# One transfer of 128 partitions in place of two of 48 for each tile's keys and queries, and another order of the passage round the last output product

## Chip, cores and metric

One core of one Trainium2 chip runs the whole program. The metric is device time in microseconds (us) of one execution, and the number that counts is the median of several.

## What is computed

1024 tokens of 512 values pass four layers, each with a residual sum and a layer norm: an attention over the 32 heads of each token by itself, a three-layer dense network, an attention with rotary embedding and a sliding window of 128 tokens, and a mixture of experts (16 experts, the best 2 per token, and a shared expert). The change lies in the third layer and in the step from it to the fourth. Cut to that:

```python
# third layer: 32 heads of 16 values, S = 1024
q, k = rope(heads(x @ Wq.T)), rope(heads(x @ Wk.T))
scores = q @ k.T / 4
scores = where((j <= i) & (j > i - 128), scores, -inf)
x = layernorm(x + (softmax(scores) @ v) @ Wo.T)
# fourth layer begins with
logits = x @ gate_w.T          # 16 experts; top 2 of softmax(logits)
```

## The kernel before

The tokens are 8 tiles (T = 8) of 128. The program is written out by hand: each engine has its own list of instructions, and semaphores tie them. Values kept in fp32 precision are split into a high and a low part (fp32r), and a product is the sum of high x high, high x low and low x high.

**Keys and queries of the third layer.** For a tile t, `rotate` and `rope_sum` (VectorE) apply the rotary embedding to one of the two products, n = 1 the keys and n = 0 the queries. `turn_rotated` (TensorE) transposes the rows, `parts_out_high` (ScalarE) and `parts_low` (VectorE) write the high and the low part. What the score products want is another layout: for each pair `pr` of 16 head pairs, one head's 16 values in three blocks (high, high, low for queries; high, low, high for keys) one below the other, 48 partitions, at partition 0 for one head and at partition 64 for the other (KS = 64). Since partitions change places, this goes through DRAM. `relay_rows` (L856) issues three stores per tile and side on SyncE's queue into `ys`, the DRAM tensor `slots_out` that the fourth layer needs only later; `stack_rows` (L1795) issues two loads per tile and side on GpSimd's queue (L1803), each of 48 partitions with 8 KB in each (384 KB), one for each half. Queries go to `qS` (three buffers, called XR and QS in the profile), keys to `kS` (four buffers, called RP). All of `kS` is set to -1 beforehand (L1792, L1830, L1838), so that the two partitions below the three blocks hold -1.

**Scores.** The main loop (L635 on TensorE) runs i from -1 to 7 with 8 steps s each. In one iteration the stages of several tiles stand side by side: `row_scores(i + 1, s)` (L562, its products are L573) for the row maxima, `key_scores(i, ...)` (L578, products L586) for the exponentials, `weigh` (L601) for softmax x values, `project2` (L515) for the products of tile i + 2, `context_rows` (L546) and `output` for tile i - 1. `row_scores(t, 0)`, the first instruction of an iteration, waits for `stack_in`, that is for the loads of the keys and the queries of tile t. VectorE takes the maxima (`row_maxima`, L1185), splits them, TensorE turns them, and `stack_maxima` (L1810, GpSimd's queue) writes them as two more partitions (48 and 49 of each half) below the queries, so that 50 rows of `qS` and `kS` give score minus maximum. `key_scores(i, 0, 0)` waits for that transfer (`max_in`). ScalarE takes the exponentials, GpSimd cuts the window out of them (`mask`, L1818 and L1821).

On GpSimd, iteration i has in step 4 a mask, then `stack_rows(i + 2, 1)`, in step 5 a mask, then `stack_rows(i + 2, 0)`, in step 6 a mask, then `stack_maxima(i + 1, 0)`, in step 7 a mask.

**From the third layer to the fourth.** After the loop the last tile's context is turned (L546, L553), its output product runs (`output(U, R, 7)`, 12 products of L515), VectorE adds it and takes the statistics (`add_output`), and every tile is normalised (`normalise`, ScalarE) and turned (`turn_x3`, L343) into XT3, split by `high_x3` (ScalarE) and `low_x3` (VectorE). `logits_turned(g)` multiplies the four tiles of group g with the gate (12 products of L332 from RP and XR). Turned tiles go through the ring V, two PSUM banks: a third one waits until VectorE has read the first. The logits decide the slots, and the fourth layer's gathers and weight loads start from those.

The profile calls helpers by their own line: L1451 is every activation, L915 every tensor_tensor, L332 every plain product, L343 a turned row of tiles.

## Time and profile before

| | us |
|---|---|
| median of 3 runs | 733.93 (730.81 to 736.4) |
| the profiled execution | 731.17 |
| its span in the trace | 729.4 |
| mean granted TensorE clock (1 is 2.4 GHz) | 0.918 |
| TensorE busy | 615.2 (84% of the span) |
| VectorE busy | 393.2 (54%) |
| ScalarE busy | 270.8 (37%) |
| GpSimd busy | 239.0 (33%) |

Times in the trace count from the start of the span. The third layer's loop runs from about 230 to 507 us, the step to the fourth layer from there to about 546 us. A row of a timeline gives the start, the duration, the engine, the line, what is written and read, how many instructions are merged, and in brackets how long the engine had been idle before it and what ended that. "<-issue" there means that the profile shows no releaser.

### The profile page before, as it was taken

How to read it: one execution, taken by the hardware profiler on the slowest of the kernel's cores; microseconds unless marked ns; L12 is line 12 of the kernel's file. 1: busy time of each engine (PE TensorE's matmuls, PEld its weight loads, DVE VectorE, ACT ScalarE, POOL GpSimd, SP SyncE). 2: the span in 40 equal slices, each digit the busy share in tenths (PEclk: the TensorE clock that was granted, in tenths of full speed). 3: DMA queues.
4: the chain of work that ended last, by engine and by line, in shares of the span. 5: the costliest groups of instructions: out<-in, count | busy, mean ns of one | idle time of the engine just before them, and what ended most of it. 6: DMA issues, size and time to landing. Idle time of an engine off the chain costs nothing.

```text
span 729.4 us, 13453 instructions
## 1 busy us (share of the span) xinstructions
PE 615.2 (84%) x5108; PEld 485.6 (67%) x5108; DVE 393.2 (54%) x1126; ACT 270.8 (37%) x433; POOL 239.0 (33%) x348
## 2 busy tenths in 40 slices
PE   2998999669889787998979896868789699999985
PEld 2987977557667565666757664645558588888762
DVE  4315445697765775767666684552464133323355
ACT  5155036366563323424243442444530112221313
POOL 6002523543310245535343552462007311111072
PEclk9999999999999886999898997577899899999998
DMA  8921211442057444618171638020007759997455
GB/s 304 392 103 27 54 34 25 104 134 74 0 145 155 106 116 61 155 23 176 35 143 46 131 110 165 2 89 3 0 1 283 279 178 409 415 418 286 185 167 193
DMA packets 49455, 104.37 MB, mean 143 GB/s; under 512 B 12208, under 2 KB 18480, under 8 KB 47856
## 3 DMA queue, kind: packets, MB, share of 16 engines
q1 hardware_dynamic: 30032, 61.68, 24.0%
q0 software_dynamic: 13744, 31.61, 18.9%
q10 hardware_dynamic: 5616, 10.23, 3.9%
q8 instruction: 41, 0.67, 0.4%
q14 instruction: 22, 0.18, 0.1%
HBM read 63.77 MB, written 35.13 MB: 136 GB/s over the span
## 4 chain that ended last, share of the span: by engine, by line
PE 53%; DMA 13%; DVE 10%; ACT 9%; issue 8%; POOL 6%; SPq 1%; POOLq 0%; ACTq 0%; DVEq 0%
PE bank L332 12%; PE bank L515 11%; PE bank L368 9%; DMA slots_out<-FP 5%; ACT FP L1451 4%; DVE FP L915 4%; PE bank L601 3%; PE bank L586 3%; PE bank L573 3%; POOL slots_in L1854 2%; POOL FP L1866 2%; DMA QS<-QS 2%; PE bank L391 2%; PE bank L546 2%; PE bank L379 1%
## 5 line engine op out<-in xcount | busy, mean ns | idle before, releaser
L1451 ACT ACTIVATE FP<-bank 128x512 f32<-128x512 f32 (+1 forms) x244 | 138.7, 611 | 316.3 <-PE bank L586 131.1
L1185 DVE CUSTOM_DVE_ANT_0 kraw<-bank,maskb 128x256 bf16<-128x256 f32 (+1 forms) x256 | 88.5, 401 | 60.1 <-PE bank L573 60.1
L515 PE MATMUL bank<-W,XR 128*128 128x512 f32 x348 | 107.0, 454 | 0.1
L332 PE MATMUL bank<-FP 128*128 128x128 f32 x558 | 89.1, 315 | 1.0 <-ACT FP L1451 1.0
L515 PEld LDWEIGHTS bank<-W,XR 128*128 128x128 f32 x348 | 72.0, 219 | 16.3 <-DVE XR L915 0.3
L368 PE MATMUL bank<-W,XR 128*128 128x512 f32 x288 | 77.6, 419 | 5.2 <-DVE W L915 5.2
L1818 POOL TENSOR_SCALAR_AFFINE_SELECT FP<-FP 128x512 f32<-128x512 f32 x64 | 41.4, 670 | 112.4 <-ACT FP L1451 112.4
L368 PEld LDWEIGHTS bank<-W,XR 128*128 128x128 f32 x288 | 64.2, 271 | 11.8 <-DVE W L915 5.6
L332 PEld LDWEIGHTS bank<-FP 128*128 128x128 f32 x558 | 66.9, 196 | 3.0 <-DVE FP L915 1.6
L915 DVE TENSOR_TENSOR FP<-FP,bank 128x128 f32<-128x128 f32 (+1 forms) x39 | 14.4, 370 | 68.4 <-ACT FP L1451 47.4
L332 PE MATMUL bank<-RP,W 128*128 128x512 f32 x192 | 45.8, 394 | 2.2 <-DVE FP L915 2.2
L1821 POOL TENSOR_SCALAR_AFFINE_SELECT FP<-FP 128x512 f32<-128x512 f32 x56 | 38.0, 705 | 29.3 <-ACT FP L1451 29.1
L1859 POOL DMA_DIRECT2D FP<-slots_in x31 | 16.7, 540 | 86.5 <-PE bank L717 79.9
L1774 POOL DMA_DIRECT2D RPF<-FP x64 | 31.5, 502 | 38.5 <-PE bank L404 27.8
L332 PEld LDWEIGHTS bank<-RP,W 128*128 128x128 f32 x192 | 35.7, 188 | 10.5 <-issue 1.8
L573 PE MATMUL bank<-RP,QS 48*128 48x256 f32 x160 | 23.7, 377 | 22.6 <-issue 11.8
L1386 DVE COPY FP<-bank 128x512 f32<-128x512 f32 x31 | 21.4, 691 | 37.4 <-PE bank L717 37.4
L601 PE MATMUL bank<-FP 128*17 128x128 f32 x960 | 37.9, 308 | 2.0 <-ACT FP L1451 1.8
L915 DVE TENSOR_TENSOR XR<-bank,XR 128x512 fp32r<-128x512 f32 x27 | 21.3, 806 | 31.6 <-ACT XR L1451 31.6
L573 PEld LDWEIGHTS bank<-RP,QS 48*128 48x128 f32 x160 | 14.7, 222 | 34.0 <-issue 24.4
L601 PEld LDWEIGHTS bank<-FP 128*17 128x17 f32 x960 | 26.6, 108 | 13.1 <-issue 6.0
L1854 POOL DMA_INDIRECT slots_in<-X,slots x16 | 16.7, 1045 | 48.1 <-issue 48.1
(168 smaller groups left out, 1019.4 us busy)
## 6 DMA issues: line engine op xcount, KB each, us to landing
FP<-in_experts_dram SPq DMA_DIRECT2D x31, 768.0 KB, 9.6
slots_out<-QS SPq DMA_DIRECT2D x48, 256.0 KB, 2.8
FP<-slots_in POOLq DMA_DIRECT2D x31, 256.0 KB, 6.5
slots_out<-FP ACTq DMA_DIRECT2D x31, 256.0 KB, 8.0
slots_in<-RP SPq DMA_DIRECT2D x7, 1024.0 KB, 13.6
RP<-slots_out POOLq DMA_DIRECT2D x16, 384.0 KB, 6.0
QS<-slots_out POOLq DMA_DIRECT2D x10, 384.0 KB, 8.3
FP<-in_shared_dram SPq DMA_DIRECT2D x4, 768.0 KB, 7.6
```

The lines of the kernel that those rows point to most:

```text
L332: mm = nc.tensor.matmul(bank, lhs, rhs, start=(n == 0), stop=(n == len(terms) - 1))
L368: mm = nc.tensor.matmul(b[:, :], *terms[m], start=(m == 0), stop=(m == 3 * DC - 1))
L515: mm = nc.tensor.matmul(b[:, :], *terms[n], start=(n == 0), stop=(n == len(terms) - 1))
L573: mm = nc.tensor.matmul(both[a][:, m, :], qS[i % 3][half(a, 3 * HD), pr, :], kS[half(a, 3 * HD), slots, pr, :], start=True, stop=True)
L601: mm = nc.tensor.matmul(weighing[32 * q:32 * q + HD + 1, (h // 4 % 4) * P:(h // 4 % 4 + 1) * P], vaug[:, (i - w) % 4, head(h), :], PT[hg % ...
L915: return nc.vector.tensor_tensor(o, a, b, op)
L1185: ins = nc.vector.tensor_tensor_reduce(masked[:, 2 * (f % 2) + m, 0:n], b[:, m, :], maskb[:, m0:m0 + n], 1.0, -BIG, ALU.add, ALU.max, hmax ...
L1451: return nc.scalar.activation(o, i, func, **kw)
L1774: nc.gpsimd.dma_start(vdiag[k % 3][32 * g:32 * g + 32, 272 * g:272 * g + 272].rearrange("p (s d) -> p s d", s=CH), vT[32 * g:32 * g + 32, ...
L1818: ins = nc.gpsimd.affine_select(out=pt, in_=pt, compare_op=ALU.is_ge, fill=0.0, base=0, pattern=[[0, 4], [1, P]], channel_multiplier=-1)
L1821: ins = nc.gpsimd.affine_select(out=pt, in_=pt, compare_op=ALU.is_ge, fill=0.0, base=-1, pattern=[[0, 4], [-1, P]], channel_multiplier=1)
L1854: nc.gpsimd.indirect_dma_start(xs, bass.IndirectOffsetOnAxis(slots[:, k, t:t + 1], 0), X[:, t, :], None).then_inc(scattered, 16)
```

## The change

**One transfer per tile and side.** The relay in DRAM gets a fourth block, so that 32 groups of three partitions become 32 groups of four, and each load is one transfer of all 128 partitions (1 MB in place of twice 384 KB). The fourth block is constant, -1 for keys and 0 for queries: GpSimd sets 32 partitions of two `kS` buffers, and SyncE stores them once into the four places of the relay (`edge_in`). The two partitions of the maxima are now 3 and 7 of each half, a partition of the fourth block each. Both score products now contract over the whole half, 64 rows, in place of 48 and 50. The settings of all of `kS` to -1 go, with two of them inside the loop.

**The passage round the last output product.** The output product of tile 7 stands ahead of all turns of x3 (before: tiles 0 and 1 were turned ahead of it). The turns alternate between ring V and ring Q, four banks in all, six tiles ahead of the first gate product in place of four. ScalarE normalises tiles 0 to 6 in a row. VectorE divides the second half of the last context ahead of the reciprocals for tiles 0 to 6.

```diff
@@ -168,10 +168,9 @@
-        relay_in = [[ys[a:a + 3 * P, :].bitcast(F32R).rearrange("(d m) n -> d (m n)", m=4) for a in (6 * P * n, 6 * P * n + 3 * P)]
-                    for n in range(2)]
-        relay = [[ys[a:a + 3 * P, :].rearrange("(x b m) n -> b x m n", b=3, m=4) for a in (6 * P * n, 6 * P * n + 3 * P)]
-                 for n in range(2)]
+        places = [[slice(4 * P * (2 * n + b), 4 * P * (2 * n + b + 1)) for b in range(2)] for n in range(2)]
+        relay_in = [[ys[rows, :].bitcast(F32R).rearrange("(d m) n -> d (m n)", m=4) for rows in of] for of in places]
+        relay = [[ys[rows, :].rearrange("(x b m) n -> b x m n", b=4, m=4) for rows in of] for of in places]
@@ -212,6 +211,10 @@
         weighing = banks[5]
+
+        def x3_ring(t):
+            return (V, Q)[t % 2]
+
         x_in = [sem(f"x_in{g}") for g in range(2)]
@@ -562,15 +566,15 @@
-                    pe.wait_ge(stack_in[1][i % 2], 32 * (i // 2 + 1))
-                    pe.wait_ge(stack_in[0][i % 2], 32 * (i // 2 + 1))
+                    pe.wait_ge(stack_in[1][i % 2], 16 * (i // 2 + 1))
+                    pe.wait_ge(stack_in[0][i % 2], 16 * (i // 2 + 1))
...
-                        mm = nc.tensor.matmul(both[a][:, m, :], qS[i % 3][half(a, 3 * HD), pr, :], kS[half(a, 3 * HD), slots, pr, :],
+                        mm = nc.tensor.matmul(both[a][:, m, :], qS[i % 3][half(a, KS), pr, :], kS[half(a, KS), slots, pr, :],
@@ -583,8 +587,8 @@
-                        mm = nc.tensor.matmul(both[a][:, m * P:(m + 1) * P], kS[half(a, 3 * HD + 2), (i - w) % 4, pr, :],
-                                              qS[i % 3][half(a, 3 * HD + 2), pr, :], start=True, stop=True)
+                        mm = nc.tensor.matmul(both[a][:, m * P:(m + 1) * P], kS[half(a, KS), (i - w) % 4, pr, :],
+                                              qS[i % 3][half(a, KS), pr, :], start=True, stop=True)
@@ -681,16 +685,16 @@
                     pe.wait_ge(x_ready, 2 * T + t + 1)
-                    transpose_row(("x3", t), X[:, t, :])
+                    transpose_row(("x3", t), X[:, t, :], x3_ring(t))
...
             turn_context(V, U, T - 1)
-            turn_x3(0, 1)
             output(U, R, T - 1)
-            turn_x3(2, 3)
+            turn_x3(*range(T - 2))
             def logits_turned(g):
-                V.drained(pe, ("x3", g * G + G - 1))
+                for t in (g * G + G - 2, g * G + G - 1):
+                    x3_ring(t).drained(pe, ("x3", t))
                 x3 = [[XT3[g][:, a, c, :] for c in range(DC)] for a in range(2)]
@@ -699,7 +703,7 @@
             logits_turned(0)
-            turn_x3(*range(G, T))
+            turn_x3(T - 2, T - 1)
             logits_turned(1)
@@ -857,7 +861,7 @@
                 if t >= 2:
-                    sp.wait_ge(stack_in[n][t % 2], 32 * (t // 2))
+                    sp.wait_ge(stack_in[n][t % 2], 16 * (t // 2))
                 for blk, l in ((0, 0), (1 + n, 0), (2 - n, 1)):
@@ -865,12 +869,17 @@
+            for n in range(2):
+                sp.wait_ge(edge_ready, n + 1)
+                for b in range(2):
+                    sp.dma_start(relay[1 - n][b][3].rearrange("x m n -> x (m n)"),
+                                 kS[0:P // 4, n].rearrange("p a k -> p (a k)").bitcast(F32)).then_inc(edge_in, 16)
             for t in range(T):
...
                     A.filled(sp, ("hidden", 1, 1, DC - 1))
-                    sp.wait_ge(stack_in[0][1], 32)
+                    sp.wait_ge(stack_in[0][1], 16)
                     load_raw(3, ao)
@@ -1286,13 +1295,13 @@
             context_divided(V, T - 1, 0)
+            context_divided(V, T - 1, 1)
             rates(slice(0, T - 1), 5)
-            context_divided(V, T - 1, 1)
             low_dense(("co", T - 1), ca[1], ca[0])
...
                 for t in tiles:
-                    low_xt(("x3", t), [XT3[t // G][:, a, :, t % G * P:(t % G + 1) * P] for a in range(2)])
+                    low_xt(("x3", t), [XT3[t // G][:, a, :, t % G * P:(t % G + 1) * P] for a in range(2)], x3_ring(t))
@@ -1304,12 +1313,12 @@
-            low_x3(0, 1)
             add_output(R, T - 1)
-            low_x3(2, 3)
+            low_x3(0)
             rates(slice(T - 1, T), 6)
+            low_x3(*range(1, T - 2))
             logits_out(0)
-            low_x3(*range(G, T))
+            low_x3(T - 2, T - 1)
             shared_low(2)
@@ -1670,21 +1679,20 @@
             def high_x3(t):
-                high_xt(("x3", t), XT3[t // G][:, 0, :, t % G * P:(t % G + 1) * P])
+                high_xt(("x3", t), XT3[t // G][:, 0, :, t % G * P:(t % G + 1) * P], x3_ring(t))
...
             normalise(0)
-            for t in range(1, G + 1):
+            for t in range(1, T - 1):
                 normalise(t)
-                high_x3(t - 1)
-            for t in range(G + 1, T - 1):
-                normalise(t)
+            high_x3(0)
+            high_x3(1)
             roots(slice(T - 1, T), 6)
...
             normalise(T - 1)
-            for t in range(G, T):
+            for t in range(2, T):
                 high_x3(t)
@@ -1789,25 +1797,22 @@
             for n in range(2):
-                nc.gpsimd.memset(kS[:, n].bitcast(F32), -1.0).then_inc(minus_ready, 1)
+                nc.gpsimd.memset(kS[0:P // 4, n].bitcast(F32), (-1.0, 0.0)[n]).then_inc(edge_ready, 1)
             def stack_rows(t, n):
...
                     Q.filled(p, ("keyscores", t - 3, 7, 1 if t >= 4 else 0))
-                if n == 1:
-                    p.wait_ge(minus_ready, min(t, 3) + 1)
-                rows = relay_in[n][t % 2]
-                for a in range(2):
-                    dst = (qS[t % 3], kS[:, t % 4])[n][KS * a:KS * a + 3 * HD]
-                    nc.gpsimd.dma_start(dst.rearrange("d a q -> d (a q)"), rows[3 * HD * a:3 * HD * a + 3 * HD]).then_inc(stack_in[n][t % 2], 16)
+                if t == 0:
+                    p.wait_ge(edge_in, 64)
+                dst = (qS[t % 3], kS[:, t % 4])[n]
+                nc.gpsimd.dma_start(dst.rearrange("d a q -> d (a q)"), relay_in[n][t % 2]).then_inc(stack_in[n][t % 2], 16)
...
                 for a in range(2):
-                    place = KS * a + 3 * HD
-                    nc.gpsimd.dma_start(qS[t % 3][place:place + 2, 8 * f:8 * f + 8, :],
+                    nc.gpsimd.dma_start(qS[t % 3][KS * a + 3:KS * a + 8:4, 8 * f:8 * f + 8, :],
                                         mxT[HD * a:HD * a + HD, f, :]).then_inc(max_in[f], 16)
@@ -1827,15 +1832,12 @@
             A.filled(p, ("ffn", T - 1))
-            nc.gpsimd.memset(kS[:, 2].bitcast(F32), -1.0).then_inc(minus_ready, 1)
             for i in range(-1, T):
...
                         nc.gpsimd.tensor_tensor(W[:, 7, :], raw_c[3], W[:, 6, :].bitcast(F32), ALU.subtract).then_inc(wo_split, 1)
-                    if (i, step) == (0, 3):
-                        nc.gpsimd.memset(kS[:, 3].bitcast(F32), -1.0).then_inc(minus_ready, 1)
                     if i >= 0 and (step % 2 == 0 or i >= 1):
```

Cut out are the ring arguments of `transpose_row`, `low_xt` and `high_xt` (the ring was always V) and the new semaphores.

GpSimd's list in one iteration (here i = 1, for tile 3; RP is `kS`, XR here `qS`), before:

```order
L1818 AFFINE_SELECT FP<-FP 128x512 x2
L1803 DMA RP<-slots_out 48x2048 x2
L1821 AFFINE_SELECT FP<-FP 128x512 x2
L1803 DMA XR<-slots_out 48x2048 x2
L1818 AFFINE_SELECT FP<-FP 128x512 x2
L1810 DMA QS<-QS 2x8x128 x2
L1821 AFFINE_SELECT FP<-FP 128x512 x2
```

and now:

```order
L1823 AFFINE_SELECT FP<-FP 128x512 x2
L1809 DMA RP<-slots_out 128x2048
L1826 AFFINE_SELECT FP<-FP 128x512 x2
L1809 DMA XR<-slots_out 128x2048
L1823 AFFINE_SELECT FP<-FP 128x512 x2
L1815 DMA QS<-QS 2x8x128 x2
L1826 AFFINE_SELECT FP<-FP 128x512 x2
```

The order is the same; each pair of loads is one load.

TensorE after the loop (from the turn of the last context, L553 before and L557 now, to the second gate product), before:

```order
L553 MATMUL bank<-ident,FP 128x128 x4
L343 MATMUL bank<-ident,X 128x128 x8
L515 MATMUL bank<-W,XR 128x512 x12
L343 MATMUL bank<-ident,X 128x128 x8
L332 MATMUL bank<-RP,XR 16x512 x12
L343 MATMUL bank<-ident,X 128x128 x16
L332 MATMUL bank<-RP,XR 16x512 x12
```

and now:

```order
L557 MATMUL bank<-ident,FP 128x128 x4
L519 MATMUL bank<-W,XR 128x512 x12
L347 MATMUL bank<-ident,X 128x128 x24
L336 MATMUL bank<-RP,XR 16x512 x12
L347 MATMUL bank<-ident,X 128x128 x8
L336 MATMUL bank<-RP,XR 16x512 x12
```

The output product moved ahead of 8 transposes (two tiles), and 8 more moved ahead of the first gate product.

VectorE there, from the first half of the last context to the sum of the output, before:

```order
L1154 RECIPROCAL hsum<-bank 128x16
L915 TENSOR_TENSOR FP<-bank,hsum 128x4x32 x2
L1045 RECIPROCAL rstd<-std 128x7
L1046 SCALAR_TENSOR_TENSOR offset<-mv,rstd 128x7
L1154 RECIPROCAL hsum<-bank 128x16
L915 TENSOR_TENSOR FP<-bank,hsum 128x4x32 x2
L915 TENSOR_TENSOR XR<-bank,XR 128x512
L1299 CAST XR<-FP 128x64
L915 TENSOR_TENSOR XR<-FP,XR 128x64
L1302 MEMSET picked 128x8
L915 TENSOR_TENSOR RP<-bank,RP 128x4x128 x2
L915 TENSOR_TENSOR X<-X,bank 128x512
```

and now:

```order
L1163 RECIPROCAL hsum<-bank 128x16
L924 TENSOR_TENSOR FP<-bank,hsum 128x4x32 x2
L1163 RECIPROCAL hsum<-bank 128x16
L924 TENSOR_TENSOR FP<-bank,hsum 128x4x32 x2
L1054 RECIPROCAL rstd<-std 128x7
L1055 SCALAR_TENSOR_TENSOR offset<-mv,rstd 128x7
L924 TENSOR_TENSOR XR<-bank,XR 128x512
L1308 CAST XR<-FP 128x64
L924 TENSOR_TENSOR XR<-FP,XR 128x64
L1311 MEMSET picked 128x8
L924 TENSOR_TENSOR X<-X,bank 128x512
```

The second division moved ahead of the reciprocals, and the two low parts of x3 moved behind the sum of the output.

## Rows read from the trace of the kernel before

**Rows 1.** Page: the chain of waits by line, share of the span.
```profile
PE bank L332 12%; PE bank L515 11%; PE bank L368 9%; DMA slots_out<-FP 5%; ACT FP L1451 4%; DVE FP L915 4%; PE bank L601 3%; PE bank L586 3%; PE bank L573 3%; POOL slots_in L1854 2%; POOL FP L1866 2%; DMA QS<-QS 2%; PE bank L391 2%; PE bank L546 2%; PE bank L379 1%
```

**Rows 2.** Waits from 184 to 512 us: who waited for whom, us, times, longest.
```profile
PE bank L573 <- issue: 15.1, 5, 6.9
...
PE bank L586 <- DMA QS<-QS: 1.3, 2, 0.7
```

**Rows 3.** Timeline of TensorE where `row_scores(t, 0)` starts, t = 2, 4, 7.
```profile
281.81 0.80 PE L573 MATMUL bank<-RP,QS 48*128 48x256 f32 x4 [2.86 <-DMA QS<-slots_out]
...
347.08 0.56 PE L573 MATMUL bank<-RP,QS 48*128 48x256 f32 x4 [2.52 <-issue]
...
452.93 0.80 PE L573 MATMUL bank<-RP,QS 48*128 48x256 f32 x4 [6.94 <-issue]
```

**Rows 4.** Timeline of GpSimd for tile 4.
```profile
335.27 1.07 POOL L1803 DMA_DIRECT2D RP<-slots_out  x2
...
337.52 1.05 POOL L1803 DMA_DIRECT2D QS<-slots_out  x2
...
341.01 1.18 POOL L1810 DMA_DIRECT2D XR<-QS  x2
```

**Rows 5.** L1803, issue to landing: keys, queries of tile 4; queries of tile 7.
```profile
DMA to landing us min/median/max: 4.8/5.7/6.6
...
DMA to landing us min/median/max: 7.3/8.1/8.9
...
DMA to landing us min/median/max: 10.8/12.9/14.9
```

**Rows 6.** Windows: five engines' busy time, TensorE's clock, mean DMA share, GB/s.
```profile
340.00:341.00 1.00, 1.00 (x13) 0.80 (x11) 0.18 (x2) 1.00 (x3) 1.00 (x2) 1.00 1.03 131
...
344.00:345.00 1.00, 0.55 (x21) 0.27 (x12) 0.96 (x2) 0.38 (x1) 0.00 (x0) 1.00 1.34 180
...
248.00:249.00 1.00, 0.00 (x0) 0.00 (x0) 0.75 (x2) 0.18 (x1) 0.28 (x1) 0.70 1.06 412
...
512.00:519.00 7.00, 6.54 (x23) 5.50 (x24) 2.27 (x7) 3.60 (x6) 0.00 (x0) 0.57 0.00 0
```

**Rows 7.** L1859, four GpSimd loads of 128 partitions issued in a row.
```profile
576.64 2.22 POOL L1859 DMA_DIRECT2D FP<-slots_in  x4 [6.65 <-DMA slots_in<-X,slots]
...
DMA to landing us min/median/max: 3.0/3.5/4.0
```

**Rows 8.** The instructions on RP: min/median/max ns, first and last start.
```profile
L586 PEld LDWEIGHTS bank<-QS,RP x320: 182/188/335, 282.2 to 502.9; 50*128 50x128 f32 x160
...
L332 PEld LDWEIGHTS bank<-RP,W x192: 186/188/192, 534.5 to 703.4; 128*128 128x128 f32 x192
...
L1803 POOL DMA_DIRECT2D RP<-slots_out x16: 512/530/551, 206.9 to 435.7; - x16
...
L1792 POOL MEMSET RP<- x2: 1812/1844/1875, 186.3 to 188.2; 128x2048 f32 x2
```

**Rows 9.** Timelines of TensorE, ScalarE and VectorE after the loop.
```profile
510.42 0.66 PE L553 MATMUL bank<-ident,FP 128*128 128x128 f32 x4 [2.08 <-DVE FP L915]
512.46 1.97 PE L343 MATMUL bank<-ident,X 128*128 128x128 f32 x8 [1.39 <-ACT X L1451]
514.08 4.84 PE L515 MATMUL bank<-W,XR 128*128 128x512 f32 x12
518.76 1.04 PE L343 MATMUL bank<-ident,X 128*128 128x128 f32 x8
530.20 2.94 PE L332 MATMUL bank<-RP,XR 128*16 128x512 f32 x12 [1.48 <-DVE RP L915]
...
511.61 1.51 ACT L1451 ACTIVATE X<-X,offset,rstd 128x512 f32<-128x512 f32 x2
...
509.28 0.20 DVE L1045 RECIPROCAL rstd<-std 128x7 f32<-128x7 f32 x1 [2.49 <-ACT std L1451]
520.51 1.46 DVE L915 TENSOR_TENSOR RP<-bank,RP 128x512 fp32r<-128x512 f32 x2
```

More of the change, by code:

```diff
@@ L930, in _, with low_xt @@
             highs = [0]
-            def low_xt(name, parts):
-                b = V.take(v, name)[:, :].rearrange("p (c n) -> p c n", c=DC)
+            def low_xt(name, parts, ring=V):
+                b = ring.take(v, name)[:, :].rearrange("p (c n) -> p c n", c=DC)
                 hi, lo = parts
```

15 lines of the change are left out of this document (8 added, 7 removed).

## The prediction

> **What bounds the kernel now.** I read the chain of waits by line first. Products on TensorE lead it: L332 12%, L515 11%, L368 9%, L586 and L573 3% each [rows 1]. So TensorE sets the pace, and the question is where it stands idle. The change touches two stretches, and each is read by itself.
>
> The first is the loop. The list of waits for it shows TensorE idle ahead of L573, the row scores, for 15.1 us in 5 waits without a named releaser, and ahead of L586, the key scores, for 1.3 us behind the transfers of the maxima [rows 2]. A sixth wait of L573, 2.86 us, ends with the landing of the queries [rows 3]. The timeline shows where the six stand: at the first product of an iteration, `row_scores(t, 0)`, for t = 2 to 7; three of them are 2.86, 2.52 and 6.94 us [rows 3]. That product waits for the loads of keys and queries of tile t. For t = 4 these loads can be followed. GpSimd issues them at 335.27 (keys, 2) and 337.52 (queries, 2) [rows 4]; the second of the last pair starts half way, at 338.05, and lands 8.9 us later [rows 5], so at 346.9. TensorE starts again at 347.08 [rows 3]. "Issue" in that row is the loads.
>
> I call the issue of the keys T0. TensorE was ready at 347.08 - 2.52 = 344.56, T0 + 9.3; the queries land at T0 + 11.7.
>
> The second stretch is the passage after the loop. TensorE waits 2.08 us for VectorE ahead of the turn of the last context and 1.39 us for ScalarE ahead of the turns of x3; only then does the output product run, in 4.84 us at a mean granted clock of 0.57 [rows 6, 9]. The second gate product starts at 530.20 [rows 9], and everything after it hangs on it, since the logits decide the slots.
>
> **The loads.** The four landings for tile 4 are 335.27 + 4.8 = 340.1, 335.81 + 6.6 = 342.4, 337.52 + 7.3 = 344.8 and 338.05 + 8.9 = 346.9 [rows 4, 5]. They are 2.3 us apart on average: one transfer of 393 KB after the other, at 173 GB/s, and 4.8 - 2.3 = 2.5 us lie ahead of the data of the first. All that time the DMA engines are busy (share 1.03 and more) and move only 131 to 180 GB/s [rows 6]. A load of 128 partitions that runs alone, the output weights on SyncE's queue, moves 412 GB/s at the same share [rows 6]. On GpSimd's own queue four loads of 262 KB and 128 partitions are issued within 2.22 us; the first lands after 3.0 us, the last, issued at about 578.3, after 4.0 us [rows 7], so 786 KB follow between 579.6 and 582.3, 291 GB/s.
>
> One new load has 1049 KB. At 412 GB/s its data take 2.5 us, at 291 GB/s 3.6 us, at 173 GB/s 6.1 us. I take 3.0 us, between the first two, as both are for all 128 partitions. The queries then land at T0 + 2.5 + 3.0 + 3.0 = T0 + 8.5 (T0 + 7.5 to T0 + 9.7), ahead of T0 + 9.3. A single issue also puts the queries' issue at T0 + 1.8 and the maxima's at T0 + 4.7 in place of T0 + 5.7 [rows 4].
>
> The Trainium skill, SBUF — State Buffer, section "Door 1: The DMA port swizzle", says that partitions 0 to 63 reach only half of the 16 ports, that two transfers to the two halves don't add up, and gives 196 GB/s for 64 and 328 GB/s for 128 partitions at 1 MiB. The 173 GB/s above agree with the first; by the second a load would take 3.2 us, the queries would land at T0 + 8.9, and the sum below would stay within half a us.
>
> The maxima follow the queries on the same queue and gate the key scores that start some 0.4 us after `row_scores(t, 0)`; behind the queries they land by T0 + 9.5 to T0 + 11, where TensorE asks for them at T0 + 9.7. I leave 0.3 us of stall per tile. Tiles 2 to 6: the waits are 2.9 + 15.1 - 6.9 + 1.3 = 12.4 us [rows 2, 3], less 5 x 0.3 = 1.5 left over, gain 10.9 us.
>
> Tile 7 is apart: its queries take up to 14.9 us to land [rows 5], because SyncE loads the shared expert's weights at the same time. From about 437.8 us the engines must then move 2.1 MB of keys and queries and 1.8 MB of weights, tables and gate. At 350 to 412 GB/s that is 9.5 to 11 us, to 447.3 to 448.8; TensorE asks at 452.93 - 6.94 = 445.99. Some 1.7 us of the 6.94 stay, gain 5.2 us (3 to 6.9).
>
> Where a stall goes, the next wait shows. During tile 4's stall VectorE works on: 0.96 us of the first microsecond [rows 6]. The first row maxima of an iteration will start about 0.4 us after the scores, and the two banks of V pass that on. Over six iterations I give back 2.0 us (0 to 5).
>
> **What else the first part does, at nothing.** GpSimd sets the constants from 186.3 on, 1.8 us each, and is done at some 190; then SyncE stores them (four stores of 256 KB), by an estimate until 195. The first stack load, which now waits for them (`edge_in`), is issued only at 206.9 [rows 8], behind the first relay, so over ten us cover them. If that cover were gone, one wide load's time, 5.5 us, would bound their cost. The two settings in the loop go, 1.8 us each on GpSimd, off the path. The stores of the relay keep their number and size; their rows lie 32 KB apart instead of 24 KB, which nothing here prices, and tile 4's were landed before its loads were issued; I count it as 0 (0 to 2). The products contract over 64 rows in place of 48 and 50. No row shows 64. A weight load takes 188 ns with 50 rows and 188 ns with 128 [rows 8], so I take 0; if time went with rows, a quarter on top of the 3% and 3% of L573 and L586 [rows 1] would be 11 us.
>
> **The passage.** Step by step with the durations of rows 9. VectorE no longer waits for ScalarE's table and roots ahead of the second division: it starts it when the context is turned, at 508.4, and ends at 509.1 in place of 510.4. The turn of the context ends at 509.8, ScalarE's high part at 510.5, VectorE's low part at 511.2. The output product starts at 511.25. At the low level of the clock it takes 4.5 us, to 515.75, against 518.9 now: 3.2 us early. Then two x3 tiles in 1.04 us, ScalarE 0.6 each, VectorE behind `add_output`, its statistics and the last rates. VectorE has the longest list: sum and statistics 1.6 us to 517.4, low part of tile 0 to 518.1, rates to 518.5, low parts of tiles 1, 2 and 3. ScalarE normalises tile 7 until 519.2 and only then takes tile 2, so tile 2's low part ends at 520.5 and tile 3's at 521.2. First gate product 521.25 to 524.2, tiles 6 and 7 through TensorE, ScalarE and VectorE (0.5 + 0.6 + 0.7 and 0.7 more), second gate product from 526.8 in place of 530.2. Gain 3.4 us. The seven normalisations in a row (some 0.7 us each) [rows 9] end at 515.4, before the first turned tile is wanted by ScalarE. If TensorE, idle for less, keeps the full clock, the output product takes 2.8 us as the gate product's 12 do [rows 9], and the gain is 5.1. If VectorE's list is longer than I have it, 2. What follows (slots, scatter, gathers, experts) starts from there and moves with it.
>
> **Sum.** -10.9 - 5.2 + 2.0 - 3.4 = -17.5 us. The profiled execution took 731.17 us, so it would take 713.7. The median of the runs is 2.8 us above the profiled one, so the forecast is 716 us. The forecast's own range: gains of 10 to 24 us, 709 to 724.
>
> **Rivals.**
> A. *Time goes with bytes.* The new loads carry 33% more. If the 173 GB/s are the way from this DRAM relay or of this queue, and not of the narrow shape, a load takes 6.1 us, the queries land at T0 + 14.7 in place of T0 + 11.7, each of tiles 2 to 6 waits 3 us longer and tile 7 some 4: +19 - 3.4, so 750 us. It decides from 5.3 us per load on. For it: no row shows a load of 128 partitions from the relay with 8 KB rows. Against it: the engines are busy at half the rate of other loads, on the same queue too [rows 6, 7]. The Trainium skill, DMA: Bandwidth & Descriptors, section "Anatomy of one DMA", has a fit of 2.0 us plus bytes over 436 GB/s whatever the shape: 0.9 us for a narrow load and 2.4 for a wide one, so a pair would lose 0.6 us. The 2.3 us between two landings speak against it. Chance 5%.
> B. *The loads get no better.* 1049 KB take as long as two narrow ones, 4.5 us. Only the passage gains: 730 to 731. Chance 7%.
> C. *The stalls go and others come.* Landings are early, but the maxima's transfer, VectorE's list or a cooler clock take half: -8 - 3 = 723 to 727. For it: VectorE is busy in most of the loop, and the maxima's margin is nil. Against it: in the stall both engines run dry. Chance 18%.
> D. The forecast, 70%.
>
> **Chances.** A measurement of this kernel tells about 1% from no change, 726.6 to 741.3. Faster by more: all of D and most of C, 0.86. Within: B, the rest of C and a little of A, 0.09. Slower: A, 0.05. The range that should hold 8 times in 10 takes in D and C: 707 to 727.
>
> **What the changed profile would show.** Loads of 128x2048 with landings of some 5.5 us for the keys, the queries landed some 8.5 us after the keys' issue, 250 GB/s and more in those windows; no wait over 0.5 us ahead of `row_scores(t, 0)` for t = 2 to 6 and one of 1 to 3 us for t = 7; the second gate product some 3.4 us nearer to the last score product. The forecast is wrong if a wide load takes over 5 us of data time, if the idle time reappears ahead of L586 or L1185's bank, or if the products of 64 rows take longer than those of 48.

## The result and the profile after

The changed kernel takes **702.38 us** (median of 4 runs, 696.95 to 709.26) beside 732.37 us of the kernel before on the same chip (4 runs, 730.17 to 736.4): a ratio of **0.956 [0.948, 0.964]**. The ratio leaves out the run of 709.26 us, in which the chip was in its slower state. The forecast was 716 us with a range of 707 to 727. The sign is right, the size is not: the gain is 30 us where 17.5 were forecast, and the time lies below the range.

The profiled execution took 700.95 us, its span is 699.2 us (before 731.17 and 729.4), so the two traces differ by 30.2 us and the medians by 30.0. The page's chain of waits by line, to be held against [rows 1]:

```profile
PE bank L336 17%; PE bank L519 11%; PE bank L372 9%; ACT FP L1460 4%; DVE FP L924 4%; PE bank L605 3%; PE bank L590 3%; PE bank L577 3%; POOL slots_in L1856 2%; PE bank L721 2%; POOL FP L1868 2%; PE bank L395 2%; DVE kraw L1194 2%; PE bank L550 2%; PE bank L383 1%
```

Line numbers have moved: L515 is now L519, the row scores L573 are L577, the key scores L586 are L590, the loads L1803 are L1809. "DMA QS<-QS", the maxima, and "DMA slots_out<-FP" have left the list.

The list of waits from 184 to 512 us, to be held against [rows 2]:

```profile
PE bank L577 <- DVE hmax L1194: 12.6, 14, 2.7
PE bank L577 <- issue: 2.7, 1, 2.7
...
PE bank L590 <- DMA XR<-QS: 1.0, 1, 1.0
```

The lists are cut to the rows of the loads and of the maxima. Five waits of 15.1 us for the loads are one of 2.7. The timeline of TensorE shows where it stands, as [rows 3] did (t = 2, 4, 7):

```profile
280.10 0.80 PE L577 MATMUL bank<-RP,QS 64*128 64x256 f32 x4 [0.75 <-DVE hmax L1194]
...
337.78 0.50 PE L577 MATMUL bank<-RP,QS 64*128 64x256 f32 x4
...
339.02 2.99 PE L519 MATMUL bank<-W,XR 128*128 128x512 f32 x12
...
424.42 0.50 PE L577 MATMUL bank<-RP,QS 64*128 64x256 f32 x4 [2.66 <-issue]
...
425.96 0.66 PE L590 MATMUL bank<-XR,RP 64*128 64x128 f32 x8 [1.05 <-DMA XR<-QS]
```

Tile 4 has no wait at all. Tile 7 still has one, and a second one for its maxima. The timeline of GpSimd for tile 4 and the landings of its keys, its queries and of tile 7's queries answer to [rows 4, 5]:

```profile
328.54 0.59 POOL L1809 DMA_DIRECT2D RP<-slots_out  x1
...
330.66 0.57 POOL L1809 DMA_DIRECT2D QS<-slots_out  x1
...
334.32 1.18 POOL L1815 DMA_DIRECT2D XR<-QS  x2
...
DMA to landing us min/median/max: 5.2/5.2/5.2
...
DMA to landing us min/median/max: 6.9/6.9/6.9
...
DMA to landing us min/median/max: 9.7/9.7/9.7
```

The keys are landed at T0 + 5.2, the queries at 330.66 + 6.9 = 337.6, T0 + 9.0, where they were at T0 + 11.7. The maxima are issued at 334.32, T0 + 5.8, as late as before (T0 + 5.7).

Now the whole loop, for which one list is not enough. The table has T0 of each tile (issue of its keys) and the start of `row_scores(t, 0)`, from the timelines of GpSimd and TensorE. "Load part" is from T0 to the row scores of the same tile, "work part" from the row scores to the next T0.

| t | row scores before | after | load part before | after | work part before | after |
|---|---|---|---|---|---|---|
| 2 | 281.81 | 280.10 | 11.90 | 9.79 | 20.54 | 20.22 |
| 3 | 314.11 | 309.54 | 11.76 | 9.22 | 21.16 | 19.00 |
| 4 | 347.08 | 337.78 | 11.81 | 9.24 | 21.99 | 18.63 |
| 5 | 380.69 | 365.78 | 11.62 | 9.37 | 22.59 | 18.85 |
| 6 | 414.91 | 393.86 | 11.63 | 9.23 | 20.23 | 18.63 |
| 7 | 452.93 | 424.42 | 17.79 | 11.93 | | |

The load parts give 17.7 us, where the forecast counted 16.1 ahead of its give-back. But the work parts, in which nothing waits for a load and for which the forecast had the 1.3 us of the maxima only, give 11.2 more (T0 of t = 2 is 0.4 later: 28.5 in all). Windows of TensorE say what they are. The columns are those of [rows 6]: the window, its length, busy time (and instructions) of TensorE's products, its weight loads, VectorE, ScalarE and GpSimd, then TensorE's granted clock, DMA share and GB/s. Before, the whole stretch from the row scores of tile 2 to those of tile 7, and 4 us behind the stall of t = 4, 5, 6 and 7:

```profile
281.81:452.93 171.12, 146.52 (x1487) 112.36 (x1488) 112.38 (x454) 61.91 (x114) 73.74 (x120) 0.90 0.49 105
...
347.08:351.08 4.00, 4.00 (x20) 3.33 (x21) 2.21 (x11) 1.09 (x2) 1.22 (x2) 0.54 0.00 0
380.69:384.69 4.00, 3.31 (x18) 2.80 (x19) 2.04 (x11) 1.09 (x2) 0.93 (x2) 0.60 0.01 2
414.91:418.91 4.00, 4.00 (x22) 3.39 (x23) 2.21 (x11) 1.08 (x2) 1.22 (x2) 0.59 0.00 0
452.93:456.93 4.00, 4.00 (x29) 3.43 (x29) 2.81 (x14) 1.09 (x2) 1.22 (x2) 0.50 0.00 0
```

And after, the same places:

```profile
280.10:424.42 144.32, 133.24 (x1488) 103.14 (x1488) 113.00 (x456) 61.89 (x114) 70.27 (x111) 0.99 0.42 142
...
337.78:341.78 4.00, 4.00 (x32) 3.32 (x28) 2.89 (x13) 1.69 (x3) 1.22 (x2) 1.00 0.03 6
365.78:369.78 4.00, 4.00 (x27) 3.35 (x28) 2.73 (x13) 1.66 (x3) 1.22 (x2) 1.00 0.01 2
393.86:397.86 4.00, 4.00 (x32) 3.32 (x28) 2.88 (x13) 1.69 (x3) 1.22 (x2) 1.00 0.01 4
424.42:428.42 4.00, 2.95 (x25) 2.27 (x26) 2.40 (x12) 1.08 (x2) 1.03 (x2) 0.81 0.04 10
```

Between the row scores of tile 2 and tile 7 the same products (1487 and 1488 records) keep TensorE busy for 13.3 us less, and it is idle for 11.1 us in place of 24.6, 13.5 less. So half of the 26.8 us is idle time, as expected, and half is the clock: after the waits of 2.3 us and more at t = 4 to 7 TensorE's granted clock was 0.50 to 0.60 in the next 4 us, near the lower level of 1.2 GHz, and where the wait is gone (t = 4 to 6) it is 1.00, that is 2.4 GHz. At t = 4 the order can be seen by the microsecond: the clock is still 1.00 in the last one of the wait (346 to 347), 0.69 in the next, in which TensorE starts again, and 0.50 in those after it, up to 354.

Whole parts of the iteration show where the 13.3 us lie. The work part of tile 4 and the load part of tile 3, before:

```profile
347.08:369.07 21.99, 20.83 (x159) 16.25 (x161) 14.95 (x60) 7.61 (x14) 7.88 (x13) 0.84 0.20 70
...
302.35:314.11 11.76, 10.36 (x143) 7.50 (x141) 7.45 (x32) 4.88 (x9) 6.87 (x13) 0.85 0.99 155
```

and after:

```profile
337.78:356.41 18.63, 17.46 (x165) 13.80 (x161) 15.62 (x62) 8.21 (x15) 7.85 (x13) 1.00 0.21 74
...
300.32:309.54 9.22, 8.80 (x145) 6.62 (x142) 6.58 (x30) 4.27 (x8) 5.91 (x11) 1.00 0.73 242
```

The work parts of tiles 3 to 6, those behind a wait for a load, keep TensorE busy for 80.0 us before and for 70.3 after, 9.7 us less. Their clock was 0.92, 0.84, 0.85 and 0.92 before and is 1.00 in all four after; by these shares the products would have lost 10.2 us, so the clock is enough to explain it. Tile 2's work part gives 0.3 us: it stands at the low level in both kernels (0.50 and 0.57 in its first 4 us). The other 3.1 us are of another kind. In the load parts of tiles 3 and 7 the clock was at 0.50 for some 3 us (from 303 and from 436), behind waits of 0.71 and 0.41 us for VectorE, which stand in nearly every iteration and mostly bring no dip, and with no wait for a load ahead. Such a dip (a short stretch at the low level) in a load part costs 1.6 us and is not bound to the stalls: experiments 3, 4, 5, 6 and 8 have one or two each, the changed kernel's trace has none. So about 10 of the 13.3 us follow the waits for the loads, and 3 may be chance.

The products that stand in the two stretches show the clock as well. The groups of TensorE's products there, before:

```profile
L515 PE MATMUL bank<-W,XR 128*128 128x512 f32 x240 | 73.8, 453 | 0.0
```

after:

```profile
L519 PE MATMUL bank<-W,XR 128*128 128x512 f32 x240 | 64.7, 408 | 0.0
```

240 of the same products keep TensorE busy for 9.1 us less, 453 ns to 408 ns each on average (they overlap).

The passage, to be held against [rows 9]; on TensorE:

```profile
481.82 0.66 PE L557 MATMUL bank<-ident,FP 128*128 128x128 f32 x4 [0.88 <-DVE FP L924]
...
483.96 4.62 PE L519 MATMUL bank<-W,XR 128*128 128x512 f32 x12 [1.48 <-DVE XR L924]
...
494.08 2.93 PE L336 MATMUL bank<-RP,XR 128*16 128x512 f32 x12 [1.59 <-DVE RP L924]
...
499.58 2.94 PE L336 MATMUL bank<-RP,XR 128*16 128x512 f32 x12 [1.69 <-DVE RP L924]
```

The wait ahead of the turn is 1.2 us shorter. From the turn to the second gate product it is 17.76 us where it was 530.20 - 510.42 = 19.78, 2.0 less.

The 30.6 us by which the second gate product is earlier are then: 1.7 at tile 2, 13.5 idle time and 13.3 clock between tiles 2 and 7, 0.1 in iteration 7 (0.7 of busy time, less 0.6 of idle time: 1.2 are saved ahead of the turn, and L590's 1.05 us for the maxima of tile 7, together with longer waits for VectorE, more than take them back), and 2.0 in the passage. 30.2 reach the end.

### The profile page after: what moved, and what is told of

Its sections match the earlier page's. It is cut to its first block, busy times and chain, and to the rows that moved or that the text cites. A ratio compares the mean times of both kernels' runs of the same rounds, so it can differ in the third digit from the quotient of the medians.

```text
span 699.2 us, 13440 instructions
## 1 busy us (share of the span) xinstructions
PE 600.9 (86%) x5108; PEld 475.4 (68%) x5108; DVE 392.0 (56%) x1126; ACT 270.5 (39%) x433; POOL 228.0 (33%) x330
## 4 chain that ended last, share of the span: by engine, by line
PE 60%; DVE 12%; ACT 9%; issue 7%; DMA 6%; POOL 5%; SPq 1%; POOLq 0%; ACTq 0%; DVEq 0%
PE bank L336 17%; PE bank L519 11%; PE bank L372 9%; ACT FP L1460 4%; DVE FP L924 4%; PE bank L605 3%; PE bank L590 3%; PE bank L577 3%; POOL slots_in L1856 2%; PE bank L721 2%; POOL FP L1868 2%; PE bank L395 2%; DVE kraw L1194 2%; PE bank L550 2%; PE bank L383 1%
## 5 line engine op out<-in xcount | busy, mean ns | idle before, releaser
L519 PE MATMUL bank<-W,XR 128*128 128x512 f32 x348 | 99.1, 427 | 1.6 <-DVE XR L924 1.5
L372 PE MATMUL bank<-W,XR 128*128 128x512 f32 x288 | 76.4, 415 | 5.2 <-DVE W L924 5.2
L519 PEld LDWEIGHTS bank<-W,XR 128*128 128x128 f32 x348 | 66.2, 201 | 16.3 <-DVE XR L924 2.0
L372 PEld LDWEIGHTS bank<-W,XR 128*128 128x128 f32 x288 | 63.6, 271 | 11.2 <-DVE W L924 5.6
L605 PE MATMUL bank<-FP 128*17 128x128 f32 x960 | 36.4, 300 | 2.0 <-ACT FP L1460 1.8
L577 PE MATMUL bank<-RP,QS 64*128 64x256 f32 x160 | 22.5, 361 | 12.0 <-DVE hmax L1194 9.1
L721 PEld LDWEIGHTS bank<-ident,FP 128*128 128x128 f32 x124 | 15.8, 145 | 21.3 <-issue 15.7
```

The source lines that it names most:

```text
L372: mm = nc.tensor.matmul(b[:, :], *terms[m], start=(m == 0), stop=(m == 3 * DC - 1))
L519: mm = nc.tensor.matmul(b[:, :], *terms[n], start=(n == 0), stop=(n == len(terms) - 1))
L577: mm = nc.tensor.matmul(both[a][:, m, :], qS[i % 3][half(a, KS), pr, :], kS[half(a, KS), slots, pr, :], start=True, stop=True)
L605: mm = nc.tensor.matmul(weighing[32 * q:32 * q + HD + 1, (h // 4 % 4) * P:(h // 4 % 4 + 1) * P], vaug[:, (i - w) % 4, head(h), :], PT[hg % ...
```

## The experiments

Three questions were open: which part brings how much; whether the clock's part is really a price of the stalls, that a stall has beyond its length; and what made the narrow loads slow (bytes, number of transfers, partitions). The kernels of experiments 1 to 4 ran on one chip, 5 and 6 on a second, 7 and 8 on a third; each is held against runs of the kernel before on its own chip, and ratios are what is compared between them.

### 1. The loads alone

The changed kernel, with the passage as before: one ring, and the order of turns and divisions of the kernel before.

```diff
-                    transpose_row(("x3", t), X[:, t, :], x3_ring(t))
+                    transpose_row(("x3", t), X[:, t, :])
...
-            turn_x3(*range(T - 2))
+            turn_x3(2, 3)
...
-            context_divided(V, T - 1, 1)
...
+            context_divided(V, T - 1, 1)
```

> The changed kernel with the passage after the loop put back as it was before. Theory: the loads took 17.7 us of stalls ahead of row_scores(t, 0) and, because TensorE then kept its full clock after each of those places, another 10.8 us, and the passage only 3.3. So this kernel is some 27 us faster than the one before (about 705), and 3 us slower than the changed one; keys' issue to row_scores(t, 0) stays 9.2 us for t = 3 to 6, and the 12 products behind context_rows take 2.75 us. Rival: the passage brought more than its 3.3 us (its clock, what starts behind it), and the loads only the 16 us that were forecast: then this kernel is at 714 or above.

Measured: 704.99 us (702.41 to 709.45, 4 runs) beside 734.43 of before (19 runs), ratio 0.964 [0.958, 0.970]. From the turn at 482.32 to the second gate product at 501.99 it is 19.67 us, as before. So most of the gain is the loads': 29.4 us, where experiment 4, which has the passage too, gains 32.1.

### 2. The passage alone

The kernel before, with two rings and the new order in the passage (the lines of experiment 1 the other way round).

> The kernel before with only the new passage after the loop; loads as before, two of 48 partitions. Theory: 3.3 us faster than before (some 0.5%), second gate product 3.3 us nearer to the last row_scores(7, 0), everything in the loop as before, with stalls of 2.3 to 2.9 us. Rival: the passage holds part of the unexplained 13 us; then it is 8 us faster or more.

Measured: 730.14 us (723.6 to 737.58, 10 runs) beside 734.43, ratio 0.994 [0.990, 0.999]. That is 4 us, 0.7 to 7.5 by the interval; 3.3 was counted. Its trace has both parts of the passage: 0.88 us of wait ahead of the turn at 517.74 where it was 2.08, and 17.73 us from there to the second gate product (535.47) where it was 19.78. The two changes add up, within what is told apart here: 29.4 + 4.3 = 33.7 beside the 32.1 of both.

### 3. Two transfers of the two halves

The changed kernel, all 64 rows stored and loaded, but in two transfers of 64 partitions each, and so with the bytes of the change and the shape of before (the counts that `stack_in` is waited for double with it).

```diff
-                nc.gpsimd.dma_start(dst.rearrange("d a q -> d (a q)"), relay_in[n][t % 2]).then_inc(stack_in[n][t % 2], 16)
+                for a in range(2):
+                    part = slice(KS * a, KS * a + KS)
+                    nc.gpsimd.dma_start(dst[part].rearrange("d a q -> d (a q)"), relay_in[n][t % 2][part]).then_inc(stack_in[n][t % 2], 16)
```

> The changed kernel, but each load is two transfers of 64 partitions, one for each half (same bytes as the changed kernel, shape as before). Theory (the narrow shape sets the rate): each half moves at some 175 GB/s, 3.0 us apart, the queries land 14.5 us after the keys' issue, stalls ahead of row_scores(t, 0) are 4.5 to 5.5 us for t = 3 to 6, the clock drops behind them, and the kernel is slower than the one before: some 745 to 750 less 3 for the passage. Rival (the number of transfers or some property of the old relay was slow, not the span of partitions): landings stay near 9 us and the time near 702 to 706.

Measured: 734.56 us (730.86 to 740.19, 10 runs), ratio 1.002 [0.998, 1.006]. The whole gain of the loads is gone, and with it what the passage brings. But the expected 742 us and more (745 to 750 less 3) were missed: I had 3.0 us between two landings. The landings of the keys issued at 370.56 and of the queries at 372.81:

```profile
DMA to landing us min/median/max: 5.5/6.5/7.4
...
DMA to landing us min/median/max: 8.0/8.8/9.6
```

The four are at 376.1, 378.5, 380.8 and 382.9 (the second of a pair is issued 0.54 us after the first), 2.3 us apart on average, as in [rows 5] (2.3), with 524 KB in place of 393 KB: about 230 GB/s in place of 173. By the distance of landings a narrow transfer took the same time with 48 partitions and with 64; the first landing is later here in most tiles (5.1 to 5.5 us where it was 4.8 to 5.2 in tiles 2 to 6).

This kernel also shows the clock. (The wait at t = 4 is the shorter one because TensorE comes to it later: its clock had a dip in the load part, as above.) The row scores of t = 4, 5 and 6 on TensorE:

```profile
351.81 0.50 PE L577 MATMUL bank<-RP,QS 64*128 64x256 f32 x4 [1.73 <-issue]
...
383.03 0.51 PE L577 MATMUL bank<-RP,QS 64*128 64x256 f32 x4 [3.19 <-issue]
...
415.99 0.80 PE L577 MATMUL bank<-RP,XR 64*128 64x256 f32 x4 [3.30 <-issue]
```

and 4 us behind each:

```profile
351.81:355.81 4.00, 4.00 (x28) 3.38 (x28) 2.12 (x11) 1.09 (x2) 1.23 (x2) 1.00 0.02 6
...
383.03:387.03 4.00, 4.00 (x23) 3.31 (x24) 2.12 (x11) 1.09 (x2) 1.22 (x2) 0.71 0.00 2
...
415.99:419.99 4.00, 4.00 (x20) 3.58 (x21) 2.21 (x11) 1.08 (x2) 1.22 (x2) 0.50 0.00 0
```

Behind the wait of 1.73 us the clock stays at 1.00 and the work part takes 18.75 us, as in the changed kernel; behind those of 3.19 and 3.30 it is 0.71 and 0.50, and the work part takes 20.38 and 21.53 us. That is the forecast's missing term inside one kernel, with one case of a short wait.

### 4. Two transfers of every other partition

As experiment 3, with the same number of transfers of the same size, but one takes the even partitions and one the odd.

```diff
-                    part = slice(KS * a, KS * a + KS)
+                    part = slice(a, P, 2)
```

> The changed kernel, but each load is two transfers of 64 partitions, the even and the odd ones, so each transfer spans the whole array with half the partitions. Theory (the span of partitions that a transfer reaches sets its rate, not how many it has): the rate stays near 350 to 400 GB/s, the queries land within 10 us of the keys' issue (half a us more for each second issue), and the time is within 3 us of the changed kernel. Rival (64 partitions in a transfer are slow wherever they lie, since fewer rows go to each engine): landings as with two halves, time 740 or more.

Measured: 702.37 us (699.94 to 704.73, 4 runs), ratio 0.957 [0.952, 0.963], the same as the change. The landings of tile 4's keys (issued at 329.31) and queries (331.62), and the rate of one microsecond between them:

```profile
DMA to landing us min/median/max: 4.0/4.9/5.8
...
DMA to landing us min/median/max: 5.0/5.5/5.9
...
333.00:334.00 1.00, 1.00 (x6) 0.81 (x5) 1.00 (x7) 0.80 (x2) 0.12 (x1) 1.00 1.16 401
```

The four landings are at 333.3, 335.7, 336.6 and 338.1. The first gap is no shorter than in experiment 3 in this tile, but in tiles 3, 5 and 6 the two keys' landings are 1.2 to 1.3 us apart; the other two gaps here are 0.9 and 1.4 us, and the engines move 401 GB/s, by which 524 KB are 1.3 us. So neither the bytes, nor the number of transfers, nor the count of partitions in one, nor the relay in DRAM as such made the loads slow: what did is which partitions a transfer covers, a block of neighbours or every other one. One thing is left: with the partitions the edit changes which rows of the relay one transfer reads, a block of 512 KB in experiment 3 and every other 8 KB here, and the two are not told apart. (One transfer of the whole 1 MB block is not slow.) Rival A of the forecast rested on the bytes or the relay, and falls here; B fell with the landings of the changed kernel.

The Trainium skill, SBUF — State Buffer, section "Door 1: The DMA port swizzle", gives the port of a partition by bits 4 to 2 and bit 6 of its number. By that rule partitions 0 to 47 and 0 to 63 both put 8 partitions on the fullest port, and 64 even partitions put 4 on each of 16. The traces agree with both: 2.3 us for 48 and for 64 neighbouring partitions, 1.3 for 64 even or odd ones.

### 5. TensorE kept busy in the stall

The kernel before, with products that nobody reads ahead of the wait for the loads, in the bank that the row scores fill next; the loads and the time at which they land stay. The wait for the bank, which stood behind the waits for the loads, now stands ahead of them. (The products add work and change no output.)

```diff
+                    for _ in range((0, 0, 10, 4, 10, 9, 9, 28)[i]):
+                        nc.tensor.matmul(banks[V.number["rowscores", i, 0] % 2][:, :], W[:, 2, 0:P], W[:, 2, 0:D], start=True, stop=True)
                     pe.wait_ge(stack_in[1][i % 2], 32 * (i // 2 + 1))
```

> The kernel before, with products that nobody reads put into the bank of the next row scores ahead of the wait for the loads: 10, 4, 10, 9, 9 and 28 of 128x512 for t = 2 to 7, some 0.23 us each at the full clock, so that TensorE is busy while the loads land. Loads and passage as before. Theory (the stall costs twice, by itself and by the clock afterwards): landings stay 11.7 us after the keys' issue, but the 12 products behind context_rows take 2.75 us in place of 3.8 to 4.9, and the kernel is 7 to 11 us faster than before although it does more work. Rival (the other 10.8 us come from something the new loads do, such as less DMA or GpSimd work ahead of the next keys' issue): no gain, within 1% of before or slower by the added products.

Measured: 725.49 us (721.68 to 729.9, 10 runs) beside 731.16 (13 runs), ratio 0.993 [0.988, 0.997]. Adding 70 useless products makes the kernel 5.7 us faster (2 to 9 by the interval). The timeline at t = 4 shows the filler, then the row scores, then the twelve products of the dense network:

```profile
346.94 2.58 PE L569 MATMUL bank<-W 128*128 128x512 f32 x10
...
349.45 0.50 PE L575 MATMUL bank<-RP,QS 48*128 48x256 f32 x4
...
350.69 3.01 PE L515 MATMUL bank<-W,XR 128*128 128x512 f32 x12
```

and 4 us behind the row scores of t = 4, 5 and 6:

```profile
349.45:353.45 4.00, 4.00 (x29) 3.32 (x28) 2.13 (x11) 1.09 (x2) 1.22 (x2) 1.00 0.02 4
379.62:383.62 4.00, 3.58 (x26) 2.96 (x26) 2.21 (x11) 1.08 (x2) 1.22 (x2) 1.00 0.01 2
410.57:414.57 4.00, 4.00 (x28) 3.32 (x28) 2.12 (x11) 1.09 (x2) 1.22 (x2) 1.00 0.00 0
```

The load parts of tiles 2 to 6 are 11.5 to 13.8 us (at t = 2 and 4 the filler ran past the landing), and the work parts of t = 2 to 6 are 18.64, 19.31, 18.64, 19.35 and 18.67 us, in sum 94.6 where they were 106.5 before and 95.3 after the change. For the question asked, tiles 3 to 6 count: TensorE's busy time in their work parts is 70.5 us here, 80.0 before and 70.3 after the change. So the clock behind the stalls comes back with the loads left as they were, by nothing but TensorE's being busy while they land, and no other effect of the new loads is needed for it. Tile 2 is a gain of the filler alone: its work part falls to 18.64 us, where the change left it at 20.22.

The gain of the whole kernel is smaller. The load parts are 1.7 us longer in sum (the dips of the clock in those of tiles 3 and 4 are still there), and tile 2 starts 2.7 us later in this trace, which is not explained. The traced execution, the fastest of the ten, is 9.5 us below the traced one of before; by the median it is 5.7, and the 7 to 11 us that I expected were too many.

### 6. The shared weights later

The changed kernel; SyncE issues the shared expert's weights only once tile 7's queries have landed, so that the two don't share the DMA engines. The gate and the table, behind them in SyncE's queue, come later with them.

```diff
             sp.wait_ge(parts_out[0], 48 * T)
+            sp.wait_ge(stack_in[0][1], 16 * (T // 2))
             load_shared(0)
```

> The changed kernel, but SyncE issues the first two loads of the shared expert's weights only when the queries of tile 7 have landed. Theory: the stall of 2.66 us ahead of row_scores(7, 0) and of 1.05 us ahead of the key scores go, queries land some 9 us after the keys' issue, the clock stays up behind them, and the kernel is 4 to 8 us faster than the changed one (695 to 699). Rival: the weights come too late for shared_high, ScalarE waits for them, and the gain is given back: within 2 us of the changed kernel.

Measured: 697.08 us (695.62 to 698.03, 4 runs) beside 731.16, ratio 0.951 [0.945, 0.958]. Tile 7's row scores on TensorE and the 4 us behind them:

```profile
422.66 0.50 PE L577 MATMUL bank<-RP,QS 64*128 64x256 f32 x4
...
422.66:426.66 4.00, 2.97 (x36) 2.38 (x32) 3.93 (x20) 2.55 (x5) 1.42 (x3) 1.00 0.77 284
```

The wait of 2.66 us and the one for the maxima are gone, the load part is 9.21 us like the others, and the clock behind it is 1.00 in place of 0.81. From these row scores to the turn of the last context (475.11) it is 52.45 us in place of 57.40, and all of that is busy time: TensorE is busy for 40.4 us in place of 45.4 and idle for 12.0 in both (waits for VectorE take the place of the one for the maxima). The shared weights, issued later, land after a median of 4.8 us in place of 7.0. Once more waits of under 4 us (2.66 + 1.05) were worth more than their length: 2.7 us in the load part and 5.0 behind it. Tile 7's T0 is 1.0 us later in this trace (the load part of tile 5 has a dip of the clock and takes 10.72 us) and the passage 0.9 longer, so the second gate product is 5.8 us earlier (493.75), and the end of the span 4.2.

### 7 and 8. The change and the later weights once more, side by side

Both kernels again, unchanged, on one chip, since the change and experiment 6 had run on different ones.

> The changed kernel once more, unaltered, on the same chip and beside the same runs of before as the next one. Theory: 0.956 of before, as measured, about 702. Rival: it lies higher or lower than that by over 1%, and single per cents between calls can't be compared.

> The changed kernel with the first two loads of the shared expert's weights issued after the queries of tile 7 have landed, beside the changed kernel on the same chip. Theory: 3 to 8 us below it (stall and clock at tile 7), clear of the interval. Rival: the 5 us seen between two calls were the chip's; then within 2 us.

Measured, beside 733.31 us of before (11 runs): the change 701.8 us (699.31 to 706.74, 6 runs), ratio 0.961 [0.955, 0.967]; the later weights 695.8 us (694.03 to 702.66, 6 runs), ratio 0.954 [0.948, 0.960]. The difference is 6.0 us. The two intervals just overlap, so "clear of the interval" was not reached, but the traces show it in the same places as above: tile 7's load part is 9.20 us in place of 11.75, and from there to the turn it is 52.94 in place of 56.76. The earlier runs (0.956 and 0.951) point the same way. The later weights are the best version of those that ran.

The second trace of the changed kernel also shows that its margin is thin: TensorE waits 0.18, 0.70 and 0.20 us for the loads of tiles 3, 4 and 6 and 1.16 us for the maxima of tile 3, where the first trace has none of these waits.

## Why the prediction was wrong, and where it was right

**The step that failed.** The part "What bounds the kernel now" names the six stalls, and the sum (in "The loads") counts each at its length ("the waits are 2.9 + 15.1 - 6.9 + 1.3 = 12.4 us"). It should have counted what TensorE does behind them as well. The clock had no term; measured it is 13.3 us of busy time between tiles 2 and 7, 9.7 of them behind the waits of tiles 3 to 6, 0.3 in tile 2 and 3.1 in two dips that no load caused. The profiled execution came out at 700.95 us where 713.7 were forecast, 12.8 less. The view that would have shown it is the one that I used for the passage alone (0.57 in [rows 6]): a window of 4 us laid behind each of the stalls of tiles 4 to 7 shows 0.54, 0.60, 0.59 and 0.50. Worse, for the loop the clock stood in the forecast on the wrong side only (for the passage a case with the full clock was priced): rival C had "a cooler clock" as something that might come, and nothing asked whether it was there already and would go. That left the lower end of the range, 707, without this case. Experiments 3, 5 and 6 show the term, each in another way.

**The loads, term by term.** Counted -10.9 and -5.2 with 2.0 given back, 14.1 us. Measured 1.7 at tile 2 and 13.5 of idle time, less the 1.05 us by which the maxima of tile 7 wait, again 14.1. That they agree to the tenth is luck, since the terms are off both ways:

- Data time of a wide load: 3.0 us assumed, queries at T0 + 8.5. They landed at T0 + 8.8 to 9.3 in tiles 3 to 6, 0.3 to 0.8 later, and just ahead of the moment at which TensorE asks (row scores at T0 + 9.2 to 9.4). The keys were earlier than counted (T0 + 5.2 to 5.3), the queries came 3.6 to 4.0 us behind them. The margin was thinner than I had it, and experiment 7 shows it used up.
- The issues: the queries' were to be at T0 + 1.8 and the maxima's at T0 + 4.7; in tile 4 they are at T0 + 2.1 and T0 + 5.8. GpSimd's mask ahead of the maxima starts at 333.14, behind a wait of 1.92 us for ScalarE, so fewer issues did not bring the maxima forward.
- 0.3 us left over per tile: in this trace nothing stayed in tiles 3 to 6, 0.75 us for VectorE at tile 2; in the second one 0.2 to 0.7 us stayed in three tiles.
- Tile 7: 1.7 us were to stay; 2.66 and 1.05 stayed. The load part is 5.9 us shorter, 5.2 counted.
- Give-back: 2.0 us. The waits of the row scores for VectorE's maxima from tile 2 on went from 3.5 to 4.3 us, which is the 0.75 of tile 2; another 0.6 us, in four short waits of L537 for VectorE, is new. Rival C (18%) did not come about.

**Products over 64 rows** cost nothing, as said (from 48 and 50 rows to 64 it is a third and 28% more, so the case in which time goes with rows would have been some 13 us, not 11): the weight loads of the key scores take the same minimum and median as in [rows 8].

```profile
L590 PEld LDWEIGHTS bank<-QS,RP x320: 182/188/335, 280.5 to 473.5; 64*128 64x128 f32 x160
...
L875 SPq DMA_DIRECT2D slots_out<-RP x4: 302/384/631, 188.3 to 190.4; - x4
```

The second row is the four stores of the constants: issued by 190.4 and landed within 4.3 us, while the first load is issued at 206.9 as before, so they are covered as priced.

**The passage.** 3.4 us counted; the traces give 1.2 ahead of the turn and 2.0 behind it, and experiment 2 gives 4 us with a wide interval and the same two numbers in its trace. The output product ran near the low level (granted clock 0.63), 4.62 us (4.5 assumed); the case in which it keeps the full clock (5.1) did not come. The gain ahead of the turn is not to be seen in the end of the changed kernel, because waits for tile 7's maxima and for VectorE take it back.

**The rivals.** A (time goes with bytes, slower) falls by experiment 4: the same bytes from the same relay, in two transfers, at 401 GB/s. B (no better than before) would have needed 4.5 us per load; the landings came 3.8 us apart (5.2, then 2.12 + 6.9), and TensorE had no wait. In the working, "173 GB/s are the narrow shape" was right; what narrow means was not known before experiments 3 and 4: the place of the partitions, not their count.

What stays open is which waits bring the low clock. Waits of 0.69 us (experiment 1, tile 5), 0.70 us (experiment 7, tile 4) and 1.73 us (experiment 3) were followed by 1.00. Before the change, t = 3 waited 0.99 us only, shortly behind a dip in its load part, and had 0.82 in the 4 us behind it and a work part 2.2 us longer than after. And t = 2 of the changed kernel has 0.57 behind a wait of 0.75 us, but there the clock was at 0.50 already from 270 us on. So the length of the wait alone does not decide. What brings the dips in the load parts was not tried either.

## What to carry to other kernels

Price a stall of TensorE as its length plus what the granted clock costs behind it, read from a window laid directly after each wait; here the second, some 10 us, was not much smaller than the 13.5 us of idle time. Compare it with the same stretch of a run without the wait, since the clock also falls where no load is waited for. Where a wait can't be removed, products that nobody reads, sized to end with it, give some of it back. Where one transfer can't cover all 128 partitions, try every other partition in place of a block. Before letting a late transfer start "early, since the queue is free", look at whose critical load it will share the engines with.

## What the runs showed of the hardware that I had not expected

- Waits of 2.3 to 3.3 us left TensorE's clock at 0.50 to 0.71 in the 4 us behind them (0.81 in one case, tile 7 of the changed kernel, behind 2.66 us). In tiles 4 to 6 each cost 1.5 to 3.7 us in the work part against the same iteration of the changed kernel without a wait; behind 1.73 us it was 1.00 (experiment 3).
- The clock also fell to 0.50 for some 3 us in the middle of an iteration, behind waits of 0.71 and 0.41 us for VectorE, at a cost of 1.6 us each; kernels with and without stalls have such dips.
- A load into 48 neighbouring partitions took as long as one into 64 (2.3 us of data with 8 KB per partition), and 64 even or odd ones little over half of that (1.3 us at 401 GB/s).
- A load of 393 KB to 48 partitions takes 2.3 us of data time. By the fit in the Trainium skill, DMA: Bandwidth & Descriptors, section "Anatomy of one DMA" (bytes over 436 GB/s), the estimate is 0.9 us, which is too low here; the measurement decides. For the wide load of 1049 KB the estimate by it is 2.4 us. The two fastest microseconds of tile 3's loads show 418 and 393 GB/s, by which it would be 2.5 to 2.7 us; but the next two show 328 and 385, and the queries landed 3.6 to 4.0 us behind the keys in tiles 3 to 6:

```profile
303.00:304.00 1.00, 1.00 (x24) 0.78 (x15) 0.23 (x1) 0.00 (x0) 0.00 (x1) 1.00 1.04 418
304.00:305.00 1.00, 1.00 (x8) 0.81 (x5) 1.00 (x7) 0.78 (x2) 0.10 (x1) 1.00 1.07 393
```
